# Four graph layers on one core: dense chunks two steps further ahead, and the mean's weights made in the first convolution

## What is computed

```
layer 0: two graph convolutions, h = x @ W; out[dst] += h[src] * dinv[src] * dinv[dst]; + b; relu between them
layer 1: x @ root + bias + sum over 8 relations of mean over the edges of that relation of (x @ W[r])[src]
layer 2: attention over the edges with one matrix per relation
layer 3: relu(sum over the edges of (x @ W[type_16])[src])
```

## Time and profile before

| | us |
|---|---|
| median of 3 runs | 3158.43 (3155.14 to 3162.38) |
| the profiled execution, its time | 3158.2 |
| its span | 3156.3 |
| order and setup | 0 to 59 |
| prefill | 59 to 529 |
| first convolution | 529 to 892 |
| second convolution | 892 to 1300 |
| mean | 1300 to 1750 |
| attention and softmax | 1750 to 2310 |
| attention's sums, then layer 3 | 2310 to 3156 |

### The profile page before, as it was taken

One profiled execution on the slowest core, in us unless ns is written; L12 is line 12 of the kernel. 1 busy time (PEld: TensorE's weight loads), 2 busy tenths in 40 slices (PEclk: granted clock), 3 DMA queues, 4 the chain that ended last, 5 costly groups with the idle time before them and its releaser, 6 DMA issues. The chain is left out here.

```text
span 3156.3 us, 51519 instructions
## 1 busy us (share of the span) xinstructions
PE 2275.9 (72%) x9863; PEld 1455.6 (46%) x9864; DVE 2337.7 (74%) x7354; ACT 1718.2 (54%) x4736; POOL 2109.8 (67%) x2070
## 2 busy tenths in 40 slices
PE   2666662777746666699999576576645599999996
PEld 1444441666645655344444333366534355444442
DVE  7999982788868888699999211133489788899996
ACT  1776893889847777566666444455468412121221
POOL 2777776777557777477776677577540277677775
PEclk9999996999968888799999799755555599999998
DMA  1666672555536566355554577799745423222221
GB/s 53 219 214 199 204 221 81 157 177 173 166 119 191 185 186 192 116 149 153 159 151 145 189 267 260 227 283 292 236 136 178 134 74 72 60 61 60 63 63 38
DMA packets 320186, 497.17 MB, mean 158 GB/s; under 512 B 65930, under 2 KB 144681, under 8 KB 320058
## 3 DMA queue, kind: packets, MB, share of 16 engines
q1 hardware_dynamic: 251130, 379.68, 37.6%
q0 software_dynamic: 68928, 116.12, 14.0%
HBM read 262.91 MB, written 236.52 MB: 158 GB/s over the span
## 5 line engine op out<-in xcount | busy, mean ns | idle before, releaser
L2173 PE MATMUL bank<-sum_masked,sum_w 128*128 128x512 f32 x1280 | 568.3, 595 | 6.7 <-DVE sum_masked L2232 6.7
L2232 DVE SCALAR_TENSOR_TENSOR sum_masked<-sum_typ,sum_col 128x512 f32<-128x512 bf16 x640 | 401.6, 685 | 18.1 <-ACT sum_col L2148 14.7
L1392 PE MATMUL bank<-mean_masked,mean_w 128*128 128x512 f32 x784 | 377.3, 613 | 17.3 <-DVE mean_masked L1483 17.1
L2173 PEld LDWEIGHTS bank<-sum_masked,sum_w 128*128 128x128 f32 x1280 | 236.4, 191 | 281.1 <-issue 210.3
L2091 POOL DMA_INDIRECT sum_rows<-t_x,m_row_int x160 | 168.0, 1050 | 191.1 <-POOLq L1124 142.6
L2113 POOL DMA_INDIRECT out_dram<-sum_new,m_last_int x196 | 219.3, 1119 | 90.0 <-issue 57.7
L1247 POOL DMA_INDIRECT mean_rows<-t_x,m_row_int x196 | 217.3, 1109 | 92.0 <-issue 59.4
L1483 DVE SCALAR_TENSOR_TENSOR mean_masked<-mean_typ,mean_col 128x512 f32<-128x512 bf16 x392 | 249.8, 679 | 16.1 <-ACT mean_col L1328 15.9
L1247 POOL DMA_INDIRECT c_rows<-t_g,m_row_int x196 | 188.4, 961 | 106.0 <-issue 57.6
L1709 POOL DMA_INDIRECT at_xs<-t_x,at_order x204 | 194.3, 953 | 91.6 <-issue 61.3
L1258 POOL DMA_INDIRECT order<-m_row_int,m_order_int x196 | 208.2, 1062 | 59.7 <-issue 59.7
(11 more groups left out here) (366 smaller groups left out, 6025.8 us busy)
## 6 DMA issues: line engine op xcount, KB each, us to landing
t_hu<-at_made SPq DMA_DIRECT2D x51, 512.0 KB, 3.8
pf_xc<-x_dram SPq DMA_DIRECT2D x98, 256.0 KB
t_g<-pf_g SPq DMA_DIRECT2D x98, 256.0 KB
t_x<-pf_x SPq DMA_DIRECT2D x98, 256.0 KB
c_dense_x<-t_x SPq DMA_DIRECT2D x98, 256.0 KB, 3.9
t_x<-c_dense_x SPq DMA_DIRECT2D x98, 256.0 KB
c_same<-p_same SPq DMA_DIRECT2D x98, 128.0 KB, 3.5
t_g<-c_new SPq DMA_DIRECT2D x49, 256.0 KB
```

Source lines behind the costliest of these rows:

```text
L1392: pe.matmul(H[q][:, :], w[:, r, :], masked[:, r % MASKS, :], start=(r == 0), stop=(r == n_rel - 1))\
L2173: pe.matmul(H[n % 2][:, :], w[:, r * D:(r + 1) * D], masked[:, r % 8, :], start=(r == 0), stop=(r == R16 - 1)).then_inc(mask_used, 1)
L2232: v.scalar_tensor_tensor(out=masked[:, r % 8, :], in0=typ[:, n % 2, :], scalar=float(r), in1=col[:, n % 2, :], op0=ALU.is_equal, op1=ALU.m ...
```

## The change

The setup counts all edges only and no longer makes the weight field. A new class `MeanWeights` loads types and flags back from DRAM in c1 and makes the weight there, on VectorE behind the dense work of the steps -2 to 7, with TensorE's transposes in steps 0 and 2 and after the last step. In both convolutions every dense call has an index two higher, and the steps start at -4.

In the setup:

```diff
-        relid = sb("relid", [QR, R8 + 1, 256])
-        cnt = sb("cnt", [QR, 2, R8 + 1, 256])
+        every = sb("every", [QR, 256])
+        cnt = sb("cnt", [QR, 2, 256])
...
-            for r in range(R8):
-                last = v.tensor_scalar(relid[:, r, :], rowf[:, T8, :], float(r), None, ALU.is_equal)
-            link(last)
...
-            for r in range(R8 + 1):
-                v.tensor_tensor_scan(cnt[:, 0, r, :], flag[:, 0, :], relid[:, r, :], 0.0, ALU.mult, ALU.add)
-                last = v.tensor_tensor_scan(cnt[:, 1, r, ::-1], flag[:, 1, ::-1], relid[:, r, ::-1], 0.0,
-                                            ALU.mult, ALU.add)
-            link(last)
...
+            v.tensor_tensor_scan(cnt[:, 0, :], flag[:, 0, :], every[:, :], 0.0, ALU.mult, ALU.add)
+            link(v.tensor_tensor_scan(cnt[:, 1, ::-1], flag[:, 1, ::-1], every[:, ::-1], 0.0, ALU.mult, ALU.add))
...
-                for r in range(R8 + 1):
-                    last = v.scalar_tensor_tensor(out=cnt[:, d, r, :], in0=through[:, d, :], scalar=carry[:, d, r:r + 1],
-                                                  in1=cnt[:, d, r, :], op0=ALU.mult, op1=ALU.add)
+                last = v.scalar_tensor_tensor(out=cnt[:, d, :], in0=through[:, d, :], scalar=carry[:, d:d + 1],
+                                              in1=cnt[:, d, :], op0=ALU.mult, op1=ALU.add)
...
-            v.tensor_tensor(cnt[:, 0, :, :], cnt[:, 0, :, :], cnt[:, 1, :, :], ALU.add).then_inc(prep, 1)
+            v.tensor_tensor(cnt[:, 0, :], cnt[:, 0, :], cnt[:, 1, :], ALU.add).then_inc(prep, 1)
...
             v.wait_ge(rooted, 1)
-            v.reciprocal(field[:, DINV_F, :], root_of[:, :])
-            link(v.tensor_tensor(cnt[:, 1, 0:R8, :], cnt[:, 0, 0:R8, :], relid[:, 0:R8, :], ALU.mult))
-            link(v.tensor_reduce(own[:, :], cnt[:, 1, 0:R8, :].rearrange("q r n -> q n r"), AX.X, ALU.add))
-            link(v.tensor_scalar(own[:, :], own[:, :], -1.0, None, ALU.add))
-            v.reciprocal(field[:, WEIGHT_F, :], own[:, :]).then_inc(lin, 1)
+            v.reciprocal(field[:, DINV_F, :], root_of[:, :]).then_inc(lin, 1)
...
-                last = pe.transpose(ps[0][0:R8 + 1, i * QR:(i + 1) * QR], ends[:, i // 2, i % 2, :], m.ident[0:QR, 0:QR])
+                last = pe.transpose(ps[0][0:1, i * QR:(i + 1) * QR], ends[:, i // 2, i % 2:i % 2 + 1], m.ident[0:QR, 0:QR])
```

The new class:

```diff
+class MeanWeights:
...
+    def load(self, sp):
+        for tile, plane in ((self.typ[:, :], self.m.type_plane[R8]), (self.flag[:, 0, :], self.m.same_plane),
+                            (self.flag[:, 1, :], self.m.next_plane)):
+            sp.dma_start(tile, plane.rearrange("(q n) -> q n", n=256)).then_inc(self.loaded, 16)
...
+    def relations(self, v):
+        v.memset(self.carryT[:, :, :], 0.0)
+        self.link(v, v.memset(self.zero[:, :], 0.0))
+        v.wait_ge(self.loaded, 48)
+        for r in range(R8):
+            v.tensor_scalar(self.relid[:, r, :], self.typ[:, :], float(r), None, ALU.is_equal)
+        v.tensor_tensor_scan(self.through[:, 0, :], self.flag[:, 0, :], self.zero[:, :], 1.0, ALU.mult, ALU.max)
+        self.link(v, v.tensor_tensor_scan(self.through[:, 1, ::-1], self.flag[:, 1, ::-1], self.zero[:, :], 1.0,
+                                          ALU.mult, ALU.max))
+        v.memset(self.flag[:, 0, 0:1], 0.0)
+        self.link(v, v.memset(self.flag[:, 1, 255:256], 0.0))
+
+    def counts(self, v, relations):
+        for r in relations:
...
+            v.tensor_tensor_scan(self.cnt[:, 0, r, :], self.flag[:, 0, :], self.relid[:, r, :], 0.0, ALU.mult, ALU.add)
+            last = v.tensor_tensor_scan(self.cnt[:, 1, r, ::-1], self.flag[:, 1, ::-1], self.relid[:, r, ::-1], 0.0,
+                                        ALU.mult, ALU.add)
+        self.link(v, last)
+
...
+        v.tensor_copy(self.ends[:, 0, 0, :], self.cnt[:, 0, :, 255])
+        v.tensor_copy(self.ends[:, 1, 0, :], self.cnt[:, 1, :, 0])
+        v.tensor_copy(self.ends[:, 0, 1, :], self.through[:, 0, 255:256].to_broadcast([QR, R8]))
+        v.tensor_copy(self.ends[:, 1, 1, :], self.through[:, 1, 0:1].to_broadcast([QR, R8])).then_inc(self.prepared, 1)
...
+    def carries(self, v, bank):
+        v.wait_ge(self.turned, 1)
+        self.link(v, v.tensor_copy(self.endT[:, :, :, :].rearrange("r a b q -> r (a b q)"), bank[0:R8, 0:4 * QR]))
+        v.tensor_tensor_scan(self.carryT[:, 0, 1:QR + 1], self.endT[:, 0, 1, :], self.endT[:, 0, 0, :], 0.0,
+                             ALU.mult, ALU.add)
+        v.tensor_tensor_scan(self.carryT[:, 1, QR - 1::-1], self.endT[:, 1, 1, ::-1], self.endT[:, 1, 0, ::-1], 0.0,
+                             ALU.mult, ALU.add).then_inc(self.prepared, 1)
+
...
+        v.wait_ge(self.turned, 2)
+        v.tensor_copy(self.carry[:, :, :].rearrange("q a r -> q (a r)"), bank[0:QR, 0:2 * R8]).then_inc(self.prepared, 1)
+        v.wait_ge(self.prepared, 3)
+
+    def add_carries(self, v, d):
+        for r in range(R8):
+            last = v.scalar_tensor_tensor(out=self.cnt[:, d, r, :], in0=self.through[:, d, :], scalar=self.carry[:, d, r:r + 1],
+                                          in1=self.cnt[:, d, r, :], op0=ALU.mult, op1=ALU.add)
+        self.link(v, last)
...
+    def both_ways(self, v):
+        self.link(v, v.tensor_tensor(self.cnt[:, 0, :, :], self.cnt[:, 0, :, :], self.cnt[:, 1, :, :], ALU.add))
...
+    def of_own_relation(self, v):
+        self.link(v, v.tensor_tensor(self.cnt[:, 1, :, :], self.cnt[:, 0, :, :], self.relid[:, :, :], ALU.mult))
...
+    def reciprocals(self, v):
+        self.link(v, v.tensor_reduce(self.own, self.cnt[:, 1, :, :].rearrange("q r n -> q n r"), AX.X, ALU.add))
+        self.link(v, v.tensor_scalar(self.own, self.own, -1.0, None, ALU.add))
+        v.reciprocal(self.own, self.own).then_inc(self.prepared, 1)
...
+    def column(self, v, bank):
+        v.wait_ge(self.turned, 3)
+        v.tensor_copy(self.m.weight_col[:, :].rearrange("p (q b) -> p b q", b=2),
+                      bank[:, 0:2 * QR].rearrange("p (b q) -> p b q", b=2))
...
+    def step(self, v, b, banks):
+
+        if b == -2:
+            self.relations(v)
+        if b == -1:
+            self.counts(v, range(R8 // 2))
+        if b == 0:
+            self.counts(v, range(R8 // 2, R8))
+            self.last_of_rows(v)
+        if b == 1:
+            self.carries(v, banks[0])
+        if b == 3:
+            self.take_carries(v, banks[1])
+            self.add_carries(v, 0)
+        if b == 4:
+            self.add_carries(v, 1)
+        if b == 5:
+            self.both_ways(v)
+        if b == 6:
+            self.of_own_relation(v)
+        if b == 7:
+            self.reciprocals(v)
+
+    def turn(self, pe, b, banks):
+        ident = self.m.ident
+        if b == 0:
+            pe.wait_ge(self.prepared, 1)
+            for i in range(4):
+                last = pe.transpose(banks[0][0:R8, i * QR:(i + 1) * QR], self.ends[:, i // 2, i % 2, :], ident[0:QR, 0:QR])
+            last.then_inc(self.turned, 1)
+        if b == 2:
+            pe.wait_ge(self.prepared, 2)
+            pe.transpose(banks[1][0:QR, 0:R8], self.carryT[:, 0, 0:QR], ident[0:R8, 0:R8])
+            pe.transpose(banks[1][0:QR, R8:2 * R8], self.carryT[:, 1, 1:QR + 1], ident[0:R8, 0:R8]).then_inc(self.turned, 1)
...
+    def turn_column(self, pe, bank):
+        pe.wait_ge(self.prepared, 4)
+        for b in range(2):
+            last = pe.transpose(bank[:, b * QR:(b + 1) * QR], self.cnt[:, 0, 0, b * TE:(b + 1) * TE], self.m.ident[0:QR, 0:QR])
+        last.then_inc(self.turned, 1)
```

In `edge_stage`:

```diff
         block = ctx.enter_context(nc.Block())
-        go = lambda eng, body: pipeline4(eng, body, -2, NB + 3, 2, 4, NB)
+        go = lambda eng, body: pipeline4(eng, body, -4 if conv else -2, NB + 3, 4 if conv else 2, 4, NB)
...
+
+            if kind == CONV1:
+                mean.load(sp)
...
                 if conv:
-                    dense.load(sp, b + 2, q)
-                    dense.store(sp, b - 3, 1 - q)
+                    dense.load(sp, b + 4, q)
+                    dense.store(sp, b - 1, 1 - q)
                 if kind == CONV2:
-                    dense.store_fourth(sp, b - 4, q)
+                    dense.store_fourth(sp, b - 2, q)
...
                 if conv:
-                    dense.roots(act, b - 2)
+                    dense.roots(act, b)
...
                 if conv:
-                    dense.columns(act, b, q)
+                    dense.columns(act, b + 2, q)
...
                 if conv:
-                    dense.second(act, b - 2, q)
+                    dense.second(act, b, q)
...
                 if kind == CONV2:
-                    dense.fourth(act, b - 3, o)
+                    dense.fourth(act, b - 1, o)
...
                 if conv:
-                    dense.times_root(pe, b - 1, o)
-                    dense.turn(pe, b, q)
+                    dense.times_root(pe, b + 1, o)
+                    dense.turn(pe, b + 2, q)
...
```

(47 more changed lines are left out.)

45 lines of the change are left out of this document (21 added, 24 removed).

## The result

The changed kernel takes 3130.45 us (median of 4 runs, 3128.68 to 3132.31), against 3158.59 for the kernel before on the same chip (4 runs): ratio 0.991, 95% interval 0.9898 to 0.9923, so 28.1 us less. The forecast was 3127.7 with a range of 3114 to 3142. The profiled execution took 3132.31 us, its span is 3130.6, against 3156.3 before.

A forecast was written before the change was run, and what follows sets the result against it. Bounds: VectorE's serial chain in the setup, a 6.74 us ScalarE-TensorE circle in the first convolution, GpSimd's descriptors in the second, then tails. 3158.4 - 27.7 + 8 - 6 - 5 = 3127.7 us, range 3114 to 3142.

The forecast's parts named there:

- Setup, 27.7: Setup: compares, scans, carry additions, sum and reciprocal work leave VectorE's serial chain, 27.7 us gained, bounds 25.5 and 28.5.
- Dense chunks ahead, -6 and -5: Tails of both convolutions lose dense work: 6 us gained in the first (3 to 8), 5 in the second (2 to 8).
- The mean's weights in the first convolution, +8: First convolution, steps -2 to 7: 31 us of added VectorE work, mostly covered, delays the loop 8 us, bounds 0 and 31.
- The hand schedule: First convolution's head: VectorE step lengths added put c_new of chunk 5 at 613.5 instead of 605.90, 7.7 us late.
- the bf16 compares: First convolution's head: 1.7 us of compares beside the first gathers; even GpSimd standing still throughout would not delay the first scan.
- Later stages: Stages after the convolutions keep their lengths; the forecast is wrong if one moves by more than 3 us.
- All hidden: Rival, first convolution: the weights' delay is under 3 us instead of 8, time 3121; chance 0.14.
- None hidden: Rival, first convolution: the weights cost 31 us instead of 8, the loop starting only after them, time 3150.7; chance 0.11.
- No gain from the dense shift: Rival, both tails: other chain work bounds them and dense work runs beside it, so no gain, time 3138.7; chance 0.10.
- The clock: Rival, first convolution: TensorE's clock falls to 1.2 GHz and stays, all 41 steps after step 8 cost 131 us, 3259; chance 0.03.

The follow-up runs named there:

- the spread one: Changed kernel with the mean's weights spread in small pieces over steps 3 to 45 of the first convolution, all its steps written out: 3118.33 us (0.9873).
- experiment 2: One part each: kernel before with only the dense chunks two steps earlier, 3146.65 us (0.9958); changed kernel with dense chunks put back, 3142.93 us (0.9946).

## Why the prediction was right, point by point

**Setup, 27.7.** Measured 27.9 and 27.7. Every price came from a row of before, and nothing took the chain's place.

**Dense chunks ahead, -6 and -5.** The second convolution gave 5.7 (408.1 to 402.4), or 6.2 by the means of two profiles, through the tail as forecast. In the first the sum was about right and its places were not. Five profiles with the dense chunks two steps ahead and the loop as it was (two of the changed kernel, the one without step 7's work, the one with TensorE kept busy and the dense shift alone) need 279.7 to 282.8 us from chunk 5 to the end, 281.3 in the mean, against 286.5 before. The tail gives 5.2 and not 6, because the last c_new now waits for a store, which I had not looked for.

Another 2.8 us come from the head, where I had forecast nothing: chunk 5 at 74.9 and 74.8 in the two kernels with the dense chunks two steps ahead and the weights in the setup, 76.9 and 78.4 before. Some 2 us of it are TensorE's clock. In step 4 TensorE idles until the gathered rows of chunk 5 are there. The windows behind that wait, in the kernel before and in the one with the dense shift alone:

```profile
574.00:579.00 5.00, 4.73 (x28) 4.76 (x29) 1.03 (x1) 2.86 (x8) 3.78 (x5) 0.66 0.29 73
```

```profile
575.00:580.00 5.00, 4.58 (x36) 3.75 (x34) 2.70 (x8) 4.49 (x16) 3.78 (x5) 1.00 0.40 87
```

Before, the eight turned pairs take 3.45 us and the W2 product 1.30; with the dense shift alone 2.02 and 1.06. The clock fell there in twelve of the fourteen profiles, after 2.4 to 5.2 us of idling. It stayed up in the two with chunk 5 at 74.9 and 74.8, after 3.15 and 3.11 us; in three others (TensorE kept busy, the weights spread, the dense chunks four steps ahead) it fell after 3.04 to 3.22. So it is not shown that the dense shift itself keeps the clock up, and this part of its gain may be luck.

**The mean's weights in the first convolution, +8.** The mechanism was right: early steps hide the work, late ones do not, and the loop never wins a delay back. The hand schedule put chunk 5 at 84.5 us after the stage's start; it came at 87.3 and 84.9. VectorE's waits between steps 0 and 7 are one of 1.6 and one of 0.6 us, where I had said none. Against the kernel before, as the sum has it, the term measures 8.5 us: 372.6 less 364.1 without the dense shift, and as much by chunk 5 (86.1 less 77.6) with it. Against the kernel with the dense shift alone it is larger, 10.8 us by the stage (367.4 less 356.6) and 11.2 by chunk 5 (86.1 less 74.9), since with the weights the clock falls in step 4 as it did before, the gathered rows of chunk 5 come later, and the 2.8 us of the head are gone. That the whole stage came close, 3.3 us longer by the means instead of 2, owes something to luck: the head gained and lost what I had not looked at.

Two things that my schedule lacked are in these numbers. One is TensorE's low clock. Turned rows and W2 product are longer by 2.6 us in step 4 and 2.5 in step 8 of the first profile, by 1.4, 1.7 and 1.5 in steps 4, 7 and 8 of the second; before it was 1.7 and 2.5 in step 4 alone. The other is GpSimd: descriptors of 0.94 us became 1.29 to 1.39 in the head, and chunk 5's first gather was issued 37.2 and 36.5 us after the stage's first descriptor in the two profiles, not 35.0. It is on the path: ScalarE waits for these rows and scales them 44.6 and 43.9 us after the stage's start, before it was 42.7 and 43.3. Three descriptors of the head, and then the compares and the first scan with the descriptors beside them, in the timeline of the changed kernel:

```profile
515.19 1.38 POOL L1363 DMA_INDIRECT c_rows<-x_dram,m_src_int  x1 [0.30 <-issue]
516.88 0.95 POOL L1363 DMA_INDIRECT c_rows<-x_dram,m_src_int  x1 [0.30 <-issue]
518.13 1.39 POOL L1363 DMA_INDIRECT c_rows<-x_dram,m_src_int  x1 [0.30 <-issue]
```

```profile
505.99 1.29 DVE L1083 TENSOR_SCALAR c_w_relid<-c_w_typ 98x256 bf16<-98x256 bf16 x8 [1.86 <-DMA c_w_flag<-p_next]
506.08 0.95 POOL L1363 DMA_INDIRECT c_rows<-x_dram,m_src_int  x1 [0.30 <-issue]
...
507.20 0.68 DVE L1084 TENSOR_TENSOR_SCAN c_w_through<-c_w_flag,c_w_zero 98x256 bf16<-98x256 bf16 x1
507.33 1.29 POOL L1363 DMA_INDIRECT c_rows<-x_dram,m_src_int  x1 [0.30 <-issue]
```

The long descriptors stand beside the weights' scans, not beside the bf16 compares, which I had named. Of the 20 descriptors ahead of chunk 5's, 5 and 3 are over 1.1 us in the two profiles of the changed kernel, 1 in the spread one, where only two scans are left in this stretch, and none in the kernels that leave the weights in the setup. The Trainium skill (SBUF — State Buffer, section "SBUF: two separate sides") names, beside the 2-port modes, a VectorE operation with two SBUF inputs as one that shuts GpSimd out of their shared port, if GpSimd's own operation reads SBUF. A scan over flags and relations has two such inputs, a gather reads its indices from SBUF, and these rows agree with that half of the rule.

**Later stages.** The prefill (0.8 to 2.0 us longer, by the pair of profiles) and the mean layer (1.7 to 3.1) were to keep their lengths; the second touches the 3 us that I had set as the limit. They are why the profiled span fell by 25.7 us only, where the stages of the change sum to 29.9; the medians differ by 28.1. The prefill is bound by GpSimd too: it runs through 344 descriptors with hardly a pause, and in the first pair of profiles these are busy for 352.5 and 353.6 us, 1.1 of the 1.8 us.

Over all kernels the prefill took 469.8 to 470.9 with the weights in the setup (5 profiles) and 469.7 to 473.1 without (9); the ranges overlap. The mean layer took 445.0 to 445.9 and 445.8 to 449.5, 1.5 us between the means. The traces show where they arise. The stage's 294 descriptors are busy 327.5 to 328.4 us in the five kernels with the weights in the setup and 328.3 to 331.9 in the nine without, and by the 41st of them, 55 to 57 us into the stage, 1.1 of the 1.5 us are there. In the changed kernel 144 and 112 of them are over 1.1 us, before it was 104 in both profiles. Why the weights' place should shift them is open; no run was spent on it.

**The rivals.** All hidden: refuted by the changed kernel, and nearly reached by another order of the same work, the spread one (3 to 4 us). None hidden: 31 us against 8.5 to 11.2. No gain from the dense shift: refuted by experiment 2. The clock: it fell, in steps 4 and 8 and in some executions in step 7, but it came back within a step each time and did not stay, as rows at 1.00 from there on show. The Trainium skill (TensorE: Matmul & The Clock Gate, Part 1) has activity release the throttle; the trace agrees, since the matmuls that ended the wait ran at 0.50 and those of the next step at 1.00.

## What to carry to other kernels

Work hidden under a loop is priced by what each iteration has to spare, not by the total: 5.7 us of VectorE work in one step cost 5 us, a low clock included, and in pieces of about a microsecond next to nothing. Before a gain is put down to idle engines, look at the granted clock in both kernels: 2 us in the head were the same matmuls at half the clock. A term measured alone can differ from the same term beside another edit, here 8.5 and 10.8 us. And before a tail is priced, ask what stands next in line: here it was a store that nobody had waited for.

## What the runs showed of the hardware that was not expected

A loop over steps costs 0.1 us a step against the same steps written out (6.84 and 6.74), in a stage paced by ScalarE and TensorE, and nothing in one paced by GpSimd. The step of the earlier trace rows was one of the written-out last ones; its 6.74 is not the loop's period.

GpSimd's indirect descriptors take 0.94 us alone and up to 1.4 beside some VectorE instructions. In the changed kernel's whole trace not one of the 300 descriptors with no VectorE instruction beside it is over 1.1 us. What matters is what VectorE runs when the descriptor begins. Of the 858 that begin while an operation with two inputs, both in SBUF, runs (tensor_tensor, scalar_tensor_tensor or a scan, within 0.1 us), 379 are over 1.1 us; of the 1198 others, 2. All fourteen traces show the same, 333 to 379 long ones against 2 to 6. Stages paced by descriptors vary with this from one execution to the next: 144 long ones and a mean layer of 448.1 us in one profile of the changed kernel, 112 and 446.9 in the other.

The granted clock can fall behind 2 to 3 us of waiting and need not. Behind the wait of step 4 it stayed at 1.00 after 3.15 us in one profile and fell to 0.50 after 2.44 in another (the weights' later operations in pieces).
